# Layer norms of batches 0 to 2 placed beside the last projection of the second attention

## The chip, the cores and the metric

The kernel runs on one core of a Trainium2 chip. A core has five engines with a queue of their own each: TensorE (PE in the rows; its weight loads PEld), VectorE (DVE), ScalarE (ACT), GpSimd (POOL), and SyncE (SP), which starts transfers. They wait for each other by semaphores only. The metric is the time of one execution on the device in microseconds (us), the median of several runs.

## What is computed

A small language-model tower over 4 batches of 512 tokens with 128 features: token embedding, first attention, a layer of product-key memory, second attention, and a layer of experts, each added to the running sum `h`. The change lies between the last two:

```python
h = h + _L1_attn_ref(_layernorm(h, axis=-1), ...)   # 8 heads of 64; out @ w_out + b_out
h = h + _L1_ffn_ref(_layernorm(h, axis=-1), ...)
# in _L1_ffn_ref, x is the layer norm of h, 16 experts, k = 64
logits = jnp.einsum('bsd,de->bse', x, gate_weight)
affinity = jax.nn.softmax(logits, axis=-1).transpose(0, 2, 1)
gating, index = jax.lax.top_k(affinity, k)
x_in = jnp.take_along_axis(x[:, None, :, :], index[..., None], axis=2)
h = jax.nn.gelu(jnp.einsum('bekd,edh->bekh', x_in, w1) + b1[None, :, None, :])
x_e = jnp.einsum('bekh,ehd->bekd', h, w2) + b2[None, :, None, :]
# gating * x_e is added at the chosen tokens
```

## The kernel before

All is written by hand, one block of code per engine; the order in the code is the order in each engine's queue. `h` stays in SBUF, 16 tiles of 128 tokens; a batch (`B` = 4, `S` = 512) is four of them (`TPB`). PSUM has eight banks: 0 and 1, `quad` (2 to 5), 6 and 7.

The second attention (`attention(a1, b, ...)`) runs over 32 units of a batch, one head and 128 rows each. For a unit, TensorE makes logits (L1295), VectorE their maximum (L717), ScalarE the exponentials (L463), GpSimd the normalising product (L364); TensorE transposes (L1097), ScalarE and VectorE take the result apart into two parts (L472, and the subtraction L730), and TensorE multiplies with the values (L1109). ScalarE copies each finished head to `oT` (L477). The three first batches are in a loop. At its tail each of them contains the layer norm of the next batch: statistics on VectorE (`ln_stats`, L689 to L694) after unit 28's subtraction, the power -0.5 on GpSimd (L356, `rstd_step`), the scaling on VectorE (`ln_scale`, L701) after unit 30's, and four transposes on TensorE (`transpose_xn`, L1084, into bank 7), which ScalarE copies (L451). Then come the head projections of the next batch, and among them the output projection of the one that is done. The fourth batch is outside the loop, without a next layer norm, and its output projection (`project1(B - 1)`, L1132 and the bias L1133, into bank 6) stands alone at the end. VectorE adds it to `h` (`residual`, L747).

The expert stage begins behind that. For each batch in turn: layer norm (`lnE`), transposes into bank 7, two copies on ScalarE, into `xnT` (L651) and `xnT_all` (L652), and gate products on TensorE (L1337), which read `xnT` and write columns of bank 6. `stats`, `mv`, `rstd`, `xn` and bank 7 are there once, so a batch's scaling waits for the transposes of the one before (`ln.ps`), and transposes wait for the copies of the one before (`lnE.sb`). Behind the four batches VectorE reads the logits (L1016) and makes their softmax with an exponential on ScalarE (L654); TensorE transposes it (L1365), and VectorE finds the top 64 in eight rounds (L1032, L1034) while TensorE goes through the 16 experts of batch 0: `up` (L1344), GELU on ScalarE (L661), `down` (L1349), the result kept in `y0`. After expert `GATED` = 9 TensorE waits for the gates, transposes them (L1376), and adds one bias product (L1357) after each of the next four experts. A loop over batches 1 to 3 follows, whose results VectorE weighs and adds to `h`.

Of the kernel before, what the change touches and what calls it, by code (L numbers as in the profile page):

```python
# [13 lines left out]
def tower(nc, x_idx, val_idx, num_rows, mask_idx, event_table, value_table, tok_w1, tok_b1, tok_w2b2,  # L14
# [7 lines left out]
    P = 128  # L22
# [26 lines left out]
    GATED = 9  # L49

    with ExitStack() as ctx:
# [396 lines left out]
        def _(act):  # L448
# [5 lines left out]
            def attention(a, b, next_ln=None):  # L454
# [24 lines left out]
                for s in range(UNITS + 9):  # L479
# [7 lines left out]
                    if s == UNITS + 4 and next_ln is not None:  # L487
                        copy_xnT(next_ln, b + 1)
# [157 lines left out]
            attention(a1, B - 1)  # L646


            for b in range(B):
                act.wait_ge(lnE.ps, b + 1)  # L650
                nc.scalar.copy(xnT[:], bank[7][:, :])  # L651
                nc.scalar.copy(xnT_all[:, b * S:(b + 1) * S], bank[7][:, :]).then_inc(lnE.sb, 1)  # L652
# [31 lines left out]
        def _(dve):  # L684
# [25 lines left out]
            def attention(a, b, next_ln=None):  # L710


                m = a.mem

# [18 lines left out]
                for s in range(UNITS + 4):  # L733
# [6 lines left out]
                    if s == UNITS and next_ln is not None:  # L740
                        ln_stats(next_ln, (b + 1) * TPB, TPB)
                    if s == UNITS + 2 and next_ln is not None:
                        ln_scale(next_ln, b + 1, (b + 1) * TPB, TPB)
# [262 lines left out]
            attention(a1, B - 1)  # L1006
# [4 lines left out]
            for b in range(B):  # L1011
                layer_norm(lnE, b, b * TPB, TPB)
# [65 lines left out]
        def _(pe):  # L1078
# [8 lines left out]
            def attention(a, b, logits, next_ln=None):  # L1087
# [26 lines left out]
                for s in range(UNITS + 8):  # L1114
# [8 lines left out]
                    if s == UNITS + 3 and next_ln is not None:  # L1123
                        transpose_xn(next_ln, b + 1)

            def project(a, b, wo, bo):
# [7 lines left out]
                last.then_inc(a.proj, 1)  # L1134
# [164 lines left out]
            def project1(b):  # L1299
                pe.wait_ge(ld_wo1, 16)  # L1300
                project(a1, b, lambda g: wo1[:, g, :], bo1[:])
# [23 lines left out]
            attention(a1, B - 1, logits1)  # L1325
            project1(B - 1)


            pe.wait_ge(ld_moe, 80)
            for b in range(B):  # L1330
                if b:
                    pe.wait_ge(lnE.sb, b)
                transpose_xn(lnE, b)
                pe.wait_ge(lnE.sb, b + 1)
                for j in range(TPB):

                    last = mm(bank[6][:, (j * B + b) * NE:(j * B + b + 1) * NE], xnT[:, j * P:(j + 1) * P], gate_w[:],  # L1337
                              start=True, stop=True)
                last.then_inc(lg_ps, 1)

# [109 lines left out]
```

## Time and profile before

| | us |
|---|---|
| median of three runs | 1363.96 |
| lowest and highest | 1362.43, 1366.89 |
| the profiled execution | 1364.92 |
| its span, first to last instruction | 1363.1 |
| TensorE busy in the span | 1091.6 |
| VectorE busy in the span | 1032.9 |
| mean granted TensorE clock (1 is full) | 0.919 |

The span is what the trace covers; times in rows are microseconds from its start. A difference of two times in the trace is a difference in the same execution.

### The profile page before, as it was taken

Reading aid. Unit: us, or ns where it says so; the run is one execution under the profiler, and the core shown is the slowest. Engines: PE = TensorE matmul, PEld = TensorE weight load, DVE = VectorE, ACT = ScalarE, POOL = GpSimd, SP = SyncE. Lnnn points to the kernel's source line nnn. Section 1 sums busy time; section 2 is a strip of 40 time slices with the busy share of each in tenths; the row PEclk is TensorE's granted clock in tenths of the full one; section 3 lists DMA queues with packets and bytes.
Section 4 is the critical chain, followed back from the end, with each engine's and each line's share of the span. In section 5 each row is a group of like instructions: output and inputs, shape, how many; then the busy total and the mean of one; then the engine's idle time right before and its main releaser. Section 6 shows DMA issues by size and latency. Waiting matters only on the chain.

```text
span 1363.1 us, 24162 instructions
## 1 busy us (share of the span) xinstructions
PE 1091.6 (80%) x7848; PEld 835.8 (61%) x7848; DVE 1032.9 (76%) x2991; ACT 689.3 (51%) x1457; POOL 643.4 (47%) x530
## 2 busy tenths in 40 slices
PE   4386785867943888888888878789999898979997
PEld 2354554545532777777777778455665655656675
DVE  4697685976828999999999997387585876844587
ACT  1484674856713344344434433277484775815433
POOL 7474361743623776876677665154260542610000
PEclk9698897998977899898899989899899899978999
DMA  3300000000000000000000001100000000000000
GB/s 78 142 1 1 0 0 0 0 0 0 1 31 1 1 2 2 2 2 2 1 2 2 1 2 40 77 1 1 0 0 0 0 0 1 1 1 1 1 8 23
DMA packets 6425, 14.63 MB, mean 11 GB/s; under 512 B 1855, under 2 KB 4482, under 8 KB 5762
## 3 DMA queue, kind: packets, MB, share of 16 engines
q1 hardware_dynamic: 5314, 11.42, 2.4%
q0 software_dynamic: 1024, 2.10, 0.6%
q8 instruction: 49, 0.80, 0.3%
q14 instruction: 38, 0.31, 0.1%
HBM read 12.47 MB, written 1.05 MB: 10 GB/s over the span
## 4 chain that ended last, share of the span: by engine, by line
issue 32%; DVE 31%; PE 25%; POOL 6%; DVEq 3%; ACT 2%; POOLq 1%; DMA 0%; ACTq 0%; SPq 0%
DVE one_u L927 6%; DVE w_v L921 5%; PE quad L1349 4%; PE quad L1097 4%; PE bank L1344 4%; DVE a_eT L730 4%; DVE i L865 3%; PE quad L1109 3%; POOL wu L346 2%; DVE vals L936 2%; DVE m L858 2%; DVE bi L883 2%; POOL a_en L364 1%; DVEq L920 1%; DVE a_negmax L717 1%
## 5 line engine op out<-in xcount | busy, mean ns | idle before, releaser
L364 POOL TENSOR_TENSOR a_en<-a_e,a_rrec 128x512 f32<-128x512 f32 x256 | 265.1, 1040 | 300.7 <-DVE a_rrec L724 282.9
L717 DVE TENSOR_REDUCE a_negmax<-bank 128x1 f32<-128x512 f32 x256 | 176.1, 691 | 44.7 <-PE bank L1295 28.3
L463 ACT ACTIVATE a_e<-bank,a_negmax 128x512 f32<-128x512 f32 x256 | 176.3, 689 | 64.2 <-DVE a_negmax L717 53.6
L1097 PE MATMUL quad<-ident,a_en 128*128 128x128 f32 x1024 | 166.4, 287 | 42.1 <-DVE a_eT L730 35.2
L1097 PEld LDWEIGHTS quad<-ident,a_en 128*128 128x128 f32 x1024 | 112.4, 145 | 135.4 <-issue 121.7
L730 DVE TENSOR_TENSOR a_eT<-quad,a_eT 128x512 fp32r<-128x512 f32 x256 | 172.6, 676 | 4.5 <-ACT a_eT L472 4.3
L1109 PE MATMUL quad<-a_eT,a_v 128*128 128x512 f32 x512 | 174.1, 431 | 1.0 <-DVE a_eT L730 0.9
L396 POOL TENSOR_TENSOR vals<-relu_in,g_sb 128x512 f32<-128x512 f32 x80 | 141.3, 1792 | 40.4 <-ACT g_sb L590 21.3
L472 ACT CAST a_eT<-quad 128x512 fp32r<-128x512 f32 x256 | 148.0, 578 | 15.2 <-PE quad L1097 15.2
L1237 PE MATMUL bank<-xnT,wd 128*128 128x128 f32 x1024 | 129.0, 283 | 3.1 <-ACT relu_in L557 1.3
L1237 PEld LDWEIGHTS bank<-xnT,wd 128*128 128x128 f32 x1024 | 121.5, 195 | 8.8 <-ACT relu_in L557 8.4
L1268 PE MATMUL bank<-wu,vals 128*128 128x128 f32 x1024 | 119.3, 278 | 4.8 <-issue 4.8
L1268 PEld LDWEIGHTS bank<-wu,vals 128*128 128x128 f32 x1024 | 117.9, 195 | 4.9 <-issue 4.9
L1257 PE MATMUL quad<-w_v,one_u 128*128 128x64 f16 x2048 | 77.6, 199 | 46.5 <-DVE one_u L927 25.4
L1257 PEld LDWEIGHTS quad<-w_v,one_u 128*128 128x128 f16 x2048 | 71.0, 101 | 59.9 <-DVE one_u L927 35.0
L927 DVE TENSOR_TENSOR one_u<-iota_u,uv 128x2048 f16<-128x2048 f16 x64 | 97.4, 1580 | 0.0
L1295 PE MATMUL bank<-a_kT,a_qT 128*128 128x512 f32 x256 | 84.8, 419 | 9.3 <-DVE a_v L998 6.9
L557 ACT ACTIVATE relu_in<-bank 128x512 f32<-128x512 f32 x128 | 75.2, 596 | 24.1 <-PE bank L1237 22.4
L1349 PEld LDWEIGHTS quad<-wu,hidT 128*128 128x128 f32 x512 | 67.6, 194 | 31.4 <-issue 27.4
L1109 PEld LDWEIGHTS quad<-a_eT,a_v 128*128 128x128 f32 x512 | 79.6, 190 | 5.9 <-DVE a_eT L730 2.4
L590 ACT COPY g_sb<-quad 128x512 f32<-128x512 f32 x16 | 9.4, 587 | 138.9 <-PE quad L1257 138.9
L661 ACT ACTIVATE hidT<-bank,b1e 128x512 f32<-128x512 f32 x64 | 44.0, 687 | 62.7 <-PE bank L1344 62.4
(210 smaller groups left out, 2023.2 us busy)
## 6 DMA issues: line engine op xcount, KB each, us to landing
wd<-in_pk_down SPq DMA_DIRECT2D x1, 2048.0 KB, 8.3
wu<-in_pk_up SPq DMA_DIRECT2D x1, 2048.0 KB, 12.8
wu<-in_moe_w SPq DMA_DIRECT2D x2, 1024.0 KB
out<-h SPq DMA_DIRECT2D x4, 256.0 KB, 2.3
wd<-in_num_rows SPq DMA_DIRECT2D x1, 512.0 KB
vals<-in_pk_wqT SPq DMA_DIRECT2D x1, 512.0 KB, 3.7
vals<-in_pk_keys SPq DMA_DIRECT2D x1, 512.0 KB, 4.6
wd<-in_a_wq SPq DMA_DIRECT2D x1, 512.0 KB
```

What stands on the lines that cost most here:

```text
L364: nc.gpsimd.tensor_tensor(m.en[:, s % 3, :], m.e[:, s % 3, :], m.rrec[:, s % 4:s % 4 + 1].to_broadcast([P, S]), ALU.mult).then_inc(a.nr, 1)
L396: nc.gpsimd.tensor_tensor(*weigh_args(t, c, k, g_sb[:, slot, :])).then_inc(vals_pool, 1)
L463: nc.scalar.activation(m.e[:, s % 3, :], bank[LOGITS[s % 3]][:, :], ACT.Exp, bias=m.negmax[:, s % 4:s % 4 + 1], accum_out=m.rowsum[:, s % ...
L472: nc.scalar.copy(m.eT[:, hd % 2, 0, :, j * P:(j + 1) * P], bank[2 + s % 2].rearrange("p (c n) -> p c n", c=TPB)).then_inc(a.hi, 1)
L717: V.tensor_reduce(m.negmax[:, s % 4:s % 4 + 1], bank[LOGITS[s % 3]][:, :], AX.X, ALU.max, negate=True).then_inc(a.mx, 1)
L730: V.tensor_tensor(part[:, 1], bank[2 + s % 2].rearrange("p (c n) -> p c n", c=TPB), part[:, 0].bitcast(F32), ALU.subtract).then_inc(a.lo, 1)
L927: V.tensor_tensor(one_u[:, c * n:(c + 1) * n], iota_u[:].unsqueeze(1).to_broadcast([P, n, NU, 2]), token_pairs(uv[:, t % 2, 0, c * GT:(c + ...
L1097: last = tp(bank[2 + s % 2][:, c * P:(c + 1) * P], m.en[:, s % 3, c * P:(c + 1) * P], ident[:])
L1109: last = mm(bank[4 + g % 2], m.v[:, c, hd, :], m.eT[:, hd % 2, part, c, :], start=(hd % a.group == 0 and c == 0 and part == 0), stop=(hd % ...
L1237: last = mm(bank[g % 2][:, q * P:(q + 1) * P], wd[:, IG * g + q, :], xnT_tile(t), start=True, stop=True)
L1257: made = mm(quad[:, 2 * (c % 2) + i // half_pair, cols], one_u[:, pair // 2, :, pair % 2], w_v[:, pair // 2, k, :, :, pair % 2].rearrange( ...
L1268: last = mm(bank[6][:, 0:D], vals[:, v, :], wu[:, v, :], start=(v == 0), stop=(v == NV - 1))
```

## The change

The last attention gets a next layer norm as well, that of batch 0 for the experts. The layer norms of batches 1 and 2 follow on VectorE's queue directly behind the attention, ahead of the residual of the last batch. On TensorE their transposes stand inside the last output projection, after its first and its third block. The layer norm of batch 3 stays behind the residual. ScalarE makes one copy per batch, straight into `xnT_all`, and the gate products read that. Those of batches 0 and 1 stand behind a wait for the residual, which still reads bank 6; then come the transposes of batch 3, and the products of batches 2 and 3. `GATED` becomes 10. GpSimd's and SyncE's queues are the same.

```diff
     LOGITS = (0, 1, 6)
-    GATED = 9
+    GATED = 10
...
-            def attention(a, b, next_ln=None):
+            def attention(a, b, next_ln=None, n=None, dst=None):
...
                     if s == UNITS + 4 and next_ln is not None:
-                        copy_xnT(next_ln, b + 1)
+                        copy_xnT(next_ln, b + 1 if n is None else n, dst=dst)
...
                 heads1(b + 1)
-            attention(a1, B - 1)
-
-
-            for b in range(B):
-                act.wait_ge(lnE.ps, b + 1)
-                nc.scalar.copy(xnT[:], bank[7][:, :])
-                nc.scalar.copy(xnT_all[:, b * S:(b + 1) * S], bank[7][:, :]).then_inc(lnE.sb, 1)
+            attention(a1, B - 1, lnE, 0, xnT_all[:, 0:S])
+
+
+            for b in range(1, B):
+                copy_xnT(lnE, b, dst=xnT_all[:, b * S:(b + 1) * S])
             act.wait_ge(lg_exp_in, 1)
...
-            def attention(a, b, next_ln=None):
+            def attention(a, b, next_ln=None, n=None):
                 m = a.mem
+                n = b + 1 if n is None else n
...
                     if s == UNITS and next_ln is not None:
-                        ln_stats(next_ln, (b + 1) * TPB, TPB)
+                        ln_stats(next_ln, n * TPB, TPB)
                     if s == UNITS + 2 and next_ln is not None:
-                        ln_scale(next_ln, b + 1, (b + 1) * TPB, TPB)
+                        ln_scale(next_ln, n, n * TPB, TPB)
...
                 heads1(b + 1, b)
-            attention(a1, B - 1)
+            attention(a1, B - 1, lnE, 0)
+            layer_norm(lnE, 1, TPB, TPB)
+            layer_norm(lnE, 2, 2 * TPB, TPB)
             residual(a1, B - 1)
...
-            for b in range(B):
-                layer_norm(lnE, b, b * TPB, TPB)
+            layer_norm(lnE, B - 1, (B - 1) * TPB, TPB)
             V.memset(aff, 0.0)
...
-            def attention(a, b, logits, next_ln=None):
+            def attention(a, b, logits, next_ln=None, n=None):
...
                     if s == UNITS + 3 and next_ln is not None:
-                        transpose_xn(next_ln, b + 1)
-
-            def project(a, b, wo, bo):
+                        transpose_xn(next_ln, b + 1 if n is None else n)
+
+            def project(a, b, wo, bo, beside=None):
...
                     last = mm(dst, ones[0:1, :], bo, start=False, stop=True)
-                last.then_inc(a.proj, 1)
+                    if j == TPB - 1:
+                        last.then_inc(a.proj, 1)
+                    elif beside is not None:
+                        beside(j)
...
-            def project1(b):
+            def project1(b, beside=None):
                 pe.wait_ge(ld_wo1, 16)
-                project(a1, b, lambda g: wo1[:, g, :], bo1[:])
+                project(a1, b, lambda g: wo1[:, g, :], bo1[:], beside)
...
                 heads1(b + 1, b)
-            attention(a1, B - 1, logits1)
-            project1(B - 1)
-
-
-            pe.wait_ge(ld_moe, 80)
-            for b in range(B):
-                if b:
+            def transpose_early(j):
+                if j in (0, 2):
+                    b = 1 + j // 2
                     pe.wait_ge(lnE.sb, b)
-                transpose_xn(lnE, b)
+                    transpose_xn(lnE, b)
+
+            attention(a1, B - 1, logits1, lnE, 0)
+            project1(B - 1, transpose_early)
+
+
+            def gate(b):
                 pe.wait_ge(lnE.sb, b + 1)
...
-                    last = mm(bank[6][:, (j * B + b) * NE:(j * B + b + 1) * NE], xnT[:, j * P:(j + 1) * P], gate_w[:],
-                              start=True, stop=True)
+                    last = mm(bank[6][:, (j * B + b) * NE:(j * B + b + 1) * NE],
+                              xnT_all[:, b * S + j * P:b * S + (j + 1) * P], gate_w[:], start=True, stop=True)
                 last.then_inc(lg_ps, 1)
+
+            pe.wait_ge(ld_moe, 80)
+            pe.wait_ge(a1.add, B)
+            gate(0)
+            gate(1)
+            pe.wait_ge(lnE.sb, B - 1)
+            transpose_xn(lnE, B - 1)
+            gate(2)
+            gate(3)
```

The order of the queues, built from both programs (`[waits ...]` names the semaphores that an instruction waits for, and line numbers are each program's own).

VectorE at the end of batch 3's attention, before: the last subtractions of the exponentials, then the residual and the layer norms.

```order
L730 TENSOR_TENSOR a_eT<-quad,a_eT 128x4x128 [waits a1_expT_hi] x4
L747 TENSOR_TENSOR h<-h,bank 128x512 [waits a1_projected]
L689 BN_STATS stats<-h 128x6 x4
L692 BN_AGGR mv<-stats 128x2 x4
L694 TENSOR_SCALAR veps<-mv 128x4
L701 TENSOR_SCALAR xn<-h,mv,rstd 128x128 [waits lnE_rstd_ready]
L701 TENSOR_SCALAR xn<-h,mv,rstd 128x128 x3
```

The same place after:

```order
L729 TENSOR_TENSOR a_eT<-quad,a_eT 128x4x128 [waits a1_expT_hi]
L687 BN_STATS stats<-h 128x6 x4
L690 BN_AGGR mv<-stats 128x2 x4
L692 TENSOR_SCALAR veps<-mv 128x4
L729 TENSOR_TENSOR a_eT<-quad,a_eT 128x4x128 [waits a1_expT_hi] x2
L699 TENSOR_SCALAR xn<-h,mv,rstd 128x128 [waits lnE_rstd_ready]
L699 TENSOR_SCALAR xn<-h,mv,rstd 128x128 x3
L729 TENSOR_TENSOR a_eT<-quad,a_eT 128x4x128 [waits a1_expT_hi]
L687 BN_STATS stats<-h 128x6 x4
L690 BN_AGGR mv<-stats 128x2 x4
L692 TENSOR_SCALAR veps<-mv 128x4
L699 TENSOR_SCALAR xn<-h,mv,rstd 128x128 [waits lnE_rstd_ready,lnE_xnT_in_psum]
```

Statistics and scaling of batch 0 now stand among the last subtractions, and batch 1 directly behind them. Batch 2 follows in the same five rows, and then:

```order
L746 TENSOR_TENSOR h<-h,bank 128x512 [waits a1_projected]
L687 BN_STATS stats<-h 128x6 x4
L690 BN_AGGR mv<-stats 128x2 x4
L692 TENSOR_SCALAR veps<-mv 128x4
L699 TENSOR_SCALAR xn<-h,mv,rstd 128x128 [waits lnE_rstd_ready,lnE_xnT_in_psum]
```

So the residual stands behind three layer norms, and one layer norm behind it.

TensorE, the second half of the last projection and what comes behind it, before (`wo`, `bo`: weights and bias of the projection):

```order
L1132 MATMUL bank<-wo,oT 128x128 x8
L1133 MATMUL bank<-bo,ones 128x128
L1132 MATMUL bank<-wo,oT 128x128 x8
L1133 MATMUL bank<-bo,ones 128x128
L1084 MATMUL bank<-ident,xn 128x128 [waits lnE_xn_ready,ld_moe]
L1084 MATMUL bank<-ident,xn 128x128 x3
L1337 MATMUL bank<-gate_w,xnT 128x16 [waits lnE_xnT_in_sbuf]
L1337 MATMUL bank<-gate_w,xnT 128x16 x3
L1084 MATMUL bank<-ident,xn 128x128 [waits lnE_xn_ready,lnE_xnT_in_sbuf]
L1084 MATMUL bank<-ident,xn 128x128 x3
```

The projection from its first block on, after:

```order
L1132 MATMUL bank<-wo,oT 128x128 [waits a1_outT_in_sbuf,ld_wo1]
L1132 MATMUL bank<-wo,oT 128x128 x7
L1133 MATMUL bank<-bo,ones 128x128
L1084 MATMUL bank<-ident,xn 128x128 [waits lnE_xn_ready,lnE_xnT_in_sbuf]
L1084 MATMUL bank<-ident,xn 128x128 x3
L1132 MATMUL bank<-wo,oT 128x128 x8
L1133 MATMUL bank<-bo,ones 128x128
L1132 MATMUL bank<-wo,oT 128x128 x8
L1133 MATMUL bank<-bo,ones 128x128
L1084 MATMUL bank<-ident,xn 128x128 [waits lnE_xn_ready,lnE_xnT_in_sbuf]
L1084 MATMUL bank<-ident,xn 128x128 x3
L1132 MATMUL bank<-wo,oT 128x128 x8
```

and directly behind it:

```order
L1133 MATMUL bank<-bo,ones 128x128
L1342 MATMUL bank<-gate_w,xnT_all 128x16 [waits lnE_xnT_in_sbuf,a1_h_added,ld_moe]
L1342 MATMUL bank<-gate_w,xnT_all 128x16 x3
L1342 MATMUL bank<-gate_w,xnT_all 128x16 [waits lnE_xnT_in_sbuf]
L1342 MATMUL bank<-gate_w,xnT_all 128x16 x3
L1084 MATMUL bank<-ident,xn 128x128 [waits lnE_xn_ready,lnE_xnT_in_sbuf]
L1084 MATMUL bank<-ident,xn 128x128 x3
L1342 MATMUL bank<-gate_w,xnT_all 128x16 [waits lnE_xnT_in_sbuf]
L1342 MATMUL bank<-gate_w,xnT_all 128x16 x3
L1342 MATMUL bank<-gate_w,xnT_all 128x16 [waits lnE_xnT_in_sbuf]
L1342 MATMUL bank<-gate_w,xnT_all 128x16 x3
L1358 MATMUL bank<-xnT_all,wu 128x512
```

Two groups of transposes moved in between the blocks of the projection (that of batch 0 stands further up, in the attention), and all gate products stand behind it, on both sides of the one group of transposes that is left there.

## Rows read from the trace of the kernel before

**Rows 1.** The page: busy us (share of the span) xinstructions.

```profile
PE 1091.6 (80%) x7848; PEld 835.8 (61%) x7848; DVE 1032.9 (76%) x2991; ACT 689.3 (51%) x1457; POOL 643.4 (47%) x530
```

**Rows 2.** Instructions in time: start, us, engine line op, operands [idle before <-releaser].

```profile
1199.25 2.02 PE L1132 MATMUL bank<-wo,oT 128*128 128x128 f32 x16 [0.77 <-ACT oT L477]
...
1208.38 0.48 PE L1133 MATMUL bank<-bo,ones 1*128 1x128 f32 x2
1208.91 0.69 DVE L747 TENSOR_TENSOR h<-h,bank 128x512 f32<-128x512 f32 x1 [12.59 <-PE bank L1133]
1209.69 0.87 DVE L689 BATCH_NORM_STATS2 stats<-h 128x6 f32<-128x128 f32 x4
...
1212.38 1.12 DVE L701 TENSOR_SCALAR xn<-h,mv,rstd 128x128 f32<-128x128 f32 x4 [1.12 <-POOL rstd L356]
...
1213.64 1.09 PE L1084 MATMUL bank<-ident,xn 128*128 128x128 f32 x4 [4.78 <-DVE xn L701]
```

**Rows 3.** Chain of waits, 1214 to 1242 us: start, us, what.

```profile
1214.77 0.59 ACT xnT L651
1215.36 0.50 ACT xnT_all L652
...
1215.89 1.89 PE bank L1337 x8
...
1227.86 1.91 PE bank L1337 x8
...
1229.78 0.43 DVE logit L1016
...
1232.99 1.12 PE bank L1365 x4
...
1239.93 0.86 PE bank L1344 x2
1240.79 0.89 PE quad L1349 x8
```

**Rows 4.** Stretches: A:B us; busy (x) PE, PEld, DVE, ACT, POOL; granted clock; DMA.

```profile
1208.90:1211.40 2.50, 0.00 (x0) 0.00 (x0) 2.11 (x10) 0.00 (x0) 0.06 (x1) 1.00 0.00 0
1211.50:1229.70 18.20, 11.41 (x49) 9.83 (x49) 8.94 (x44) 4.29 (x8) 3.87 (x4) 0.50 0.00 0
...
1233.00:1238.70 5.70, 5.70 (x16) 3.96 (x17) 3.59 (x7) 2.52 (x4) 0.00 (x0) 0.50 0.01 3
1238.80:1256.00 17.20, 17.20 (x103) 12.76 (x101) 9.31 (x19) 12.64 (x20) 0.00 (x0) 1.00 0.00 0
```

**Rows 5.** Instructions in time, tail of batch 2's attention.

```profile
1107.89 2.04 POOL L364 TENSOR_TENSOR a_en<-a_e,a_rrec 128x512 f32<-128x512 f32 x2 [0.68 <-DVE a_rrec L724]
...
1109.67 0.86 DVE L689 BATCH_NORM_STATS2 stats<-h 128x6 f32 x4
...
1113.38 0.69 DVE L730 TENSOR_TENSOR a_eT<-quad,a_eT 128x512 fp32r<-128x512 f32 x1
...
1113.53 0.66 PE L1084 MATMUL bank<-ident,xn 128*128 128x128 f32 x4
...
1114.20 2.13 PE L1109 MATMUL quad<-a_eT,a_v 128*128 128x512 f32 x8
```

**Rows 6.** Instructions in time, tail of batch 3's attention.

```profile
1191.42 2.04 POOL L364 TENSOR_TENSOR a_en<-a_e,a_rrec 128x512 f32<-128x512 f32 x2 [0.68 <-DVE a_rrec L724]
...
1196.37 2.11 PE L1109 MATMUL quad<-a_eT,a_v 128*128 128x512 f32 x8 [0.47 <-DVE a_eT L730]
```

**Rows 7.** Instructions in time: the gates, and the transposes that wait for them.

```profile
1248.30 0.69 DVE L1038 TENSOR_TENSOR gT<-gT,affT 128x512 f32<-128x512 f32 x1
...
1253.78 0.60 PE L1376 MATMUL bank<-ident,gT 128*128 128x128 f32 x4
```

**Rows 8.** TensorE behind three idle pieces, and the clock of stretches after them.

```profile
974.68 1.87 PE L1295 MATMUL bank<-a_kT,a_qT 128*128 128x512 f32 x6 [1.86 <-DVE a_v L998]
...
976.00:982.50 6.50, 5.99 (x20) 3.90 (x19) 4.17 (x11) 4.74 (x12) 4.07 (x4) 0.50 0.00 0
...
1059.73 1.60 PE L1295 MATMUL bank<-a_kT,a_qT 128*128 128x512 f32 x6 [1.84 <-DVE a_v L998]
...
1061.30:1068.00 6.70, 5.91 (x20) 4.35 (x20) 4.37 (x12) 4.85 (x13) 4.18 (x5) 0.50 0.00 0
...
1144.70 1.65 PE L1295 MATMUL bank<-a_kT,a_qT 128*128 128x512 f32 x6 [1.62 <-DVE a_v L998]
...
1144.80:1150.00 5.20, 3.95 (x19) 2.60 (x20) 3.44 (x8) 3.43 (x9) 2.77 (x3) 1.00 0.00 0
```

## The prediction, made before the changed kernel ran

> **What bounds the kernel now.** I began with the page: TensorE is busy for 80% of a span of 1363.1 us, so no engine is full everywhere, and a change of this size has to be read in its own stretch [rows 1]. The views of 1190 to 1240 us come next, where the second attention ends and the expert stage begins. The last projection runs from 1199.25 to 1208.86 us, in four blocks of 16 matmul records and two bias records, 9.61 us in all, so 2.40 us a block [rows 2]. Behind it nothing overlaps. VectorE adds the residual at 1208.91, then computes the statistics of batch 0, GpSimd raises them to the power (VectorE waits 1.12 us for it), VectorE scales, and TensorE gets its first transpose at 1213.64, after 4.78 us without work [rows 2]. The chain of waits then repeats one pattern four times, once a batch, of which the first and the last are shown: transposes, two copies on ScalarE, gate products (1.89 us for four, x8 in the records) [rows 3]. Batches 1 to 3 follow in 3.99 us each (1227.86 - 1215.89, over three), and the layer norms of these batches lie beside that pattern; it is transposes, copies and gate products that end last. The logits are read at 1229.78, and their softmax ends when TensorE transposes it at 1232.99 [rows 3]. From there on the stage is one unbroken TensorE sequence of 1.75 us per expert (0.86 up, 0.89 down) [rows 3], so what is won before it moves the end of the kernel with it.
>
> The table of stretches adds the clock [rows 4]. The granted clock is 1.00 until 2.5 us behind the projection, 0.50 (the 1.2 GHz level instead of 2.4 GHz) all through transposes and gate products, and 1.00 again only 5.7 us after the softmax. So the stretch between projection and experts runs at the low level, and it stands between two long waits.
>
> **Removed.** From the end of the projection to the end of the last gate product: 1229.77 - 1208.86 = 20.91 us [rows 2, 3]. Of this all goes that belongs to batches 0 to 2, as far as something else covers it.
>
> **What stays behind the projection.** The residual, the layer norm of batch 3 and its transposes still hang on it, as batch 0's did: 4.78 us of wait, then 1.10 us for four transposes at the low clock. Products of batches 0 and 1 now stand in front of those transposes. They wait for the residual, because they write the bank that it reads: about 0.8 us behind the projection, then 2 x 0.99 us at full clock (a block's 16 matmul records take 2.02 us, 8 gate records half of that, less a little [rows 2]), or 2 x 1.89 at the low one. Both fit into the 4.78 us (0.8 + 3.8 = 4.6), so they cost nothing; without that cover they would cost 2.0 to 3.8 us. Products of batch 2 follow at once and hide the one copy that ScalarE still has to make for batch 3 (0.59 us). Products of batch 3 end the stretch. Sum at the low clock: 4.78 + 1.10 + 0.05 + 1.89 + 1.89 = 9.71 us instead of 20.91, so **-11.2 us**. The second copy and the extra reader of `xnT` that go are inside this sum; on their own they would have been worth 0.50 us in each batch [rows 3], but for batch 3 the products of batch 2 lie over them.
>
> **What the moved work costs in front.** Batch 0's layer norm now sits in the tail of the last attention, just as the layer norm for the heads of batch 3 sits in the tail of batch 2's attention. That tail is in the trace, and so is the last one, which has no layer norm [rows 5, 6]. I lay both on the last pair of GpSimd products (1107.89 and 1191.42, 83.53 us apart). With the layer norm the last eight attention records end at 1114.20 + 2.13 = 1116.33, which is 1199.86 in the later frame; without it they ended at 1196.37 + 2.11 = 1198.48. The reason is the row of VectorE: statistics at 1109.67 stand in front of two subtractions of the exponentials, and the scaling in front of the last one (1113.38), for which TensorE waits. The four transposes (0.66 us at 1113.53) fall into that wait. So the projection starts **+1.38 us** later.
>
> Inside the projection TensorE now does two groups of four transposes, after blocks 0 and 2: 2 x 0.65 = **+1.30 us**, at full clock [rows 5]. They have to be ready: VectorE is free at 1113.38 + 0.69 + 83.53 = 1197.6, statistics and power of batch 1 take 2.69 us (1209.69 to 1212.38 in rows 2), scaling 1.12, so batch 1 is ready at 1201.5, while TensorE comes to it at 1200.63 + 2.40 = 1203.0. Slack 1.5 us. Batch 2 needs `xn` free, so it waits for these transposes (1203.7), and is ready at 1205.3; TensorE comes to it at 1208.5. Slack 3.2 us. ScalarE copies between them and has nothing else to do. The residual stands behind both layer norms on VectorE, and those are over 6 us before the projection ends, so nobody waits for that. GpSimd is through with its products at 1191.42 + 2.04 = 1193.46, over 1 us before the statistics of batch 0 are there; no product or DMA stands behind its loop of four.
>
> **No cost.** The gate products read the same numbers from another tile, with equal shapes. `GATED` 10 moves the transposes of the gates one expert back: the gates are ready at 1248.30 + 0.69 = 1248.99, and TensorE came for them at 1253.78, so the wait was empty by 4.8 us, and with 10 by 6.5 [rows 7]. Their rows stay as many, and the four bias terms end one expert before the last. Were the clock to return at once after the softmax, TensorE would be there 2.8 us earlier and still find them.
>
> **Sum.** -11.2 + 1.38 + 1.30 = **-8.5 us**. The profiled execution took 1364.92 us (span 1363.1), the median of the three runs is 1363.96, so 1.0 us lower; a difference carries over, and the forecast is 1363.96 - 8.5 = 1355.5 us.
>
> **The clock, weighed.** The sum has the low level in it, and the new program shortens the wait that brought it: behind the projection TensorE now idles 0.8 us, works, idles 4.78 - 0.8 - 2.0 = 2.0 us in front of the transposes, and later some 2.3 us during the softmax (3.21 us from 1229.78 to 1232.99, less 0.86 for the first expert product at full clock). In the trace idle pieces of 1.86 and 1.84 us were followed by a fall: after 974.68 and 1059.73 the clock is 1.00 and then 0.50 for 6.5 us; one of 1.62 us, before 1144.70, was not [rows 8]. So 2.0 and 2.3 us, close together, should bring it down once at least, and I take the low level from in front of batch 3's transposes. The Trainium skill, TensorE: Matmul & The Clock Gate, section "Why this matters for your kernels", asks only that TensorE not stand still between bursts for longer than a length which neither of these pieces reaches; by that rule the clock stays at its full level, and the time is that of the first rival. Rows 8 speak against the page here.
> How long the low level lasts past the softmax is open from both sides. Before it was 5.7 us, all of it TensorE work that took twice its time, worth 2.8 us. A return at once gives -2.8; the longest stretch that rows 8 show, 6.7 us, gives +0.5. The position of a fall or a rise is not something that this change sets, so I take 5.7 again, as the nearest row of the same work.
>
> **Rivals.**
> 1. *The clock never falls.* Transposes 0.66 instead of 1.10, gate products 0.99 twice instead of 1.89, so 2.2 us, and 2.8 us behind the softmax: -8.5 - 2.2 - 2.8 = -13.5, 1350.5 us. If it falls only in the softmax, -10.7, 1353.3 us. For: both idle pieces are far shorter than 4.78. Against: rows 8.
> 2. *The tail of the attention pays more.* VectorE's queue holds statistics, a wait for GpSimd and the scaling in front of subtractions, and in the last batch there is no following projection of heads to take up slack. If a whole layer norm shows (3.8 us from 1209.69 to the end of the scaling, [rows 2]) and not 1.38, then -8.5 + 2.4 = -6.1, 1357.9 us. For: each subtraction is waited for. Against: the tail in rows 5 has the same queue, and pays 1.38.
> 3. *Slower: the projection stalls and loses the clock.* TensorE takes its queue in order, so blocks 1 to 3 stand behind batch 1's transposes. If batch 1 is not ready 1.5 us after my time, TensorE idles; if it idles by some 1.85 us more, the clock falls as in rows 8, and the remaining 7.2 us of projection take 14.4. Cost 1.85 + 7.2 + 0.4 for the second transposes = 9.5, so +1.0 net, 1365.0 us, and over that for each us of lateness. It decides from 3.4 us of lateness in all. Nothing in the trace makes the same chain of 3.8 us take 7.2, so this is remote.
> 4. *It does not do what it says.* The end of the logits might hang on something else than the four batches. The chain has no other link there [rows 3], so no change, 1364 us, is left a small chance.
>
> **How the numbers follow.** Forecast 0.70 (1355.5, its own range 1353.5 to 1357 by the bounds of the clock); rival 1 at full 0.07 and with a late fall 0.08; rival 2 0.10; rival 3 0.02; rival 4 0.03. The three runs of before spread by 4.5 us, and a median by perhaps 1, so I widen a little: 1351.5 to 1358.2 leaves out the full-clock case, rivals 3 and 4, and some spread of the rest. A difference of 0.3%, 4.1 us, is about what a measurement of this kernel can tell from none. Faster than 1359.9: forecast and rivals 1 and 2, 0.94 (with 0.01 off for spread). Same: 0.04. Slower: 0.02.
>
> **What would show it.** In the changed profile: the last projection starts about 1.4 us later and lasts 10.9 instead of 9.6 us, with no idle piece inside it; from its end to the last gate product 9.7 us, with 4.8 us from its end to batch 3's transposes; the granted clock 0.50 before these transposes and until some 5.7 us after the softmax; the wait for the gates still empty; 1.75 us for each expert as before. A stretch of 7.5 us instead of 9.7 says that the clock held. A projection that starts over 2 us later says rival 2, an idle piece inside it rival 3. I am wrong altogether if the softmax does not come about 8.5 us earlier, or if the time from there to the end grows.

## The result and the profile after

The changed kernel took 1354.97 us (median of five runs, 1353.12 to 1356.15) against 1363.96 us: 0.9928 of before, with a 95% interval of 0.991 to 0.9947. The same two kernels on another occasion gave 1355.27 against 1364.23 us, 0.9931 (0.9915 to 0.9946). So it is faster by 0.7%, 9.0 us by the medians on both occasions, where 8.5 were forecast.

The timeline of the changed kernel from the last attention to the experts (columns as in [rows 2]):

```profile
1189.52 2.04 POOL L364 TENSOR_TENSOR a_en<-a_e,a_rrec 128x512 f32<-128x512 f32 x2 [0.67 <-DVE a_rrec L723]
...
1195.16 0.66 PE L1084 MATMUL bank<-ident,xn 128*128 128x128 f32 x4
...
1195.76 2.09 PE L1109 MATMUL quad<-a_eT,a_v 128*128 128x512 f32 x8
...
1198.62 2.02 PE L1132 MATMUL bank<-wo,oT 128*128 128x128 f32 x16 [0.77 <-ACT oT L477]
...
1200.99 0.66 PE L1084 MATMUL bank<-ident,xn 128*128 128x128 f32 x4
...
1201.48 1.95 PE L1132 MATMUL bank<-wo,oT 128*128 128x128 f32 x16
...
1206.17 0.66 PE L1084 MATMUL bank<-ident,xn 128*128 128x128 f32 x4
...
1206.66 1.95 PE L1132 MATMUL bank<-wo,oT 128*128 128x128 f32 x16
...
1208.54 0.48 PE L1133 MATMUL bank<-bo,ones 1*128 1x128 f32 x2
1209.07 0.69 DVE L746 TENSOR_TENSOR h<-h,bank 128x512 f32<-128x512 f32 x1 [5.78 <-PE bank L1133]
...
1209.86 1.93 PE L1342 MATMUL bank<-gate_w,xnT_all 128*128 128x16 f32 x16 [0.83 <-issue]
...
1213.87 1.09 PE L1084 MATMUL bank<-ident,xn 128*128 128x128 f32 x4 [2.08 <-DVE xn L699]
```

The groups of transposes (L1084) now stand in the attention's tail and between the blocks of the projection, and no row of the projection has an idle piece in front but its first. The row at 1213.87 shows where the rest of the time is: TensorE idle for 2.08 us, waiting for batch 3's layer norm.

The chain of waits behind it, for [rows 3]:

```profile
1213.87 1.09 PE bank L1084 x4
1214.96 3.24 PE bank L1342 x16
...
1218.22 0.42 DVE logit L1016
...
1221.42 1.12 PE bank L1379 x4
...
1228.39 0.86 PE bank L1358 x2
1229.25 0.89 PE quad L1363 x8
```

One group of transposes and two sets of gate products, where there were four of each, and the same 3.20 us of softmax. An expert takes 0.86 + 0.89 us as before. And the clock, for [rows 4]:

```profile
1209.10:1213.50 4.40, 1.93 (x16) 1.86 (x16) 2.97 (x14) 0.00 (x0) 1.01 (x1) 1.00 0.00 0
1213.60:1221.40 7.80, 6.21 (x22) 4.66 (x22) 2.97 (x8) 2.29 (x3) 0.00 (x0) 0.50 0.00 1
1221.50:1227.10 5.60, 5.60 (x16) 3.89 (x17) 3.59 (x7) 2.45 (x4) 0.00 (x0) 0.50 0.01 3
1227.30:1244.00 16.70, 16.70 (x100) 12.36 (x99) 9.23 (x18) 12.14 (x19) 0.00 (x0) 1.00 0.00 0
```

It fell at about 1213.5, just ahead of the last transposes, and came back 5.8 us behind the start of the softmax's transposes (1221.42).

The two executions had drifted apart by 1.9 us when they reached this place, for reasons that lie before it, where the programs are the same. The differences are therefore counted from a mark that both have, the start of the last pair of GpSimd products (1191.42 and 1189.52). Times are in us:

| stretch | before | after | difference | forecast |
|---|---|---|---|---|
| mark to first projection product | 7.83 | 9.10 | +1.27 | +1.38 |
| projection | 9.61 | 10.40 | +0.79 | +1.30 |
| its end to the reading of the logits | 20.92 | 9.20 | -11.72 | -11.2 |
| logits to the softmax's transposes | 3.21 | 3.20 | 0.0 | 0 |
| from there to the end | 130.11 | 129.88 | -0.2 | 0 |
| sum | | | -9.9 | -8.5 |

### The profile page after: what moved, and what is told of

Same layout as the page of the kernel before. It is cut to its first block, busy times and chain, and to the rows that moved or that the text cites. A ratio compares the mean times of both kernels' runs of the same rounds, so it can differ in the third digit from the quotient of the medians.

```text
span 1351.3 us, 24158 instructions
## 1 busy us (share of the span) xinstructions
PE 1084.5 (80%) x7848; PEld 830.7 (61%) x7848; DVE 1033.9 (77%) x2991; ACT 686.1 (51%) x1453; POOL 643.4 (48%) x530
## 4 chain that ended last, share of the span: by engine, by line
issue 32%; DVE 32%; PE 24%; POOL 6%; DVEq 3%; ACT 2%; POOLq 1%; DMA 0%; ACTq 0%; SPq 0%
DVE one_u L926 6%; DVE w_v L920 5%; PE quad L1363 4%; PE quad L1097 4%; PE bank L1358 4%; DVE a_eT L729 4%; DVE i L864 3%; PE quad L1109 3%; POOL wu L346 2%; DVE vals L935 2%; DVE m L857 2%; DVE bi L882 2%; POOL a_en L364 1%; DVEq L919 1%; DVE a_negmax L716 1%
## 5 line engine op out<-in xcount | busy, mean ns | idle before, releaser
L1298 PE MATMUL bank<-a_kT,a_qT 128*128 128x512 f32 x256 | 81.4, 404 | 9.6 <-DVE a_v L997 6.9
```

## Experiments

All are read by the same stretches, in one profiled execution each. Two times are given: from the mark (the last pair of GpSimd products) to the softmax's transposes, 31.90 us in the changed kernel, and from there to the end, 129.88 us. In a second trace of the changed kernel they were 31.93 and 129.83 us. That is much closer than whole times, which spread by 3 to 5 us and more, and on some occasions lay 8 to 12 us higher for all kernels. The second time moves with the clock, though: it depends on how long the low level lasts behind the softmax.

### GATED back to 9

```diff
-    GATED = 10
+    GATED = 9
```

> The changed kernel with GATED back at 9; nothing else differs. My theory: the gates are ready before TensorE asks for them at 9 as at 10, so the time from the softmax's transposes to the end stays at 129.9 us (within 0.5), and the transposes of the gates start 20.8 us behind the softmax's transposes with no wait of over 0.3 us in front, instead of 22.5. Rival: the top-64 search is late for expert 9 now, TensorE waits there, and the stretch to the end grows by that wait, 1 us or more.

To the softmax's transposes 31.93 us, from there to the end 128.89, so 1.0 us less than with 10. The gates and the transposes that wait for them:

```profile
1248.72 0.69 DVE L1038 TENSOR_TENSOR gT<-gT,affT 128x512 f32<-128x512 f32 x1
...
1252.99 0.60 PE L1390 MATMUL bank<-ident,gT 128*128 128x128 f32 x4
```

Ready 3.6 us early, and no idle piece, so 9 would have done as well. My 0.5 us was missed by the clock, not by `GATED`:

```profile
1233.50:1236.60 3.10, 3.10 (x9) 2.06 (x10) 1.34 (x3) 1.49 (x3) 0.00 (x0) 0.50 0.02 5
1236.70:1254.00 17.30, 17.30 (x102) 12.76 (x102) 11.53 (x24) 12.54 (x21) 0.00 (x0) 1.00 0.00 0
```

It came back 3.3 us behind the softmax's transposes here (1233.41) and not 5.8. Expert products take twice their time at the low level (1.71 us for 0.86 in the chain of the changed kernel), so half of the difference is gained, 1.3 us, which is more than the whole 1.0 us.

The low stretch is as long as in the changed kernel, 13.7 us in both; it lies 2.5 us earlier. It begins at about 1223.0, while TensorE is in the gate products of batches 0 and 1, whose row is 2.50 us long for 1.93 in the changed kernel:

```profile
1221.83 2.50 PE L1342 MATMUL bank<-gate_w,xnT_all 128*128 128x16 f32 x16 [0.83 <-issue]
1225.85 1.09 PE L1084 MATMUL bank<-ident,xn 128*128 128x128 f32 x4 [1.51 <-DVE xn L699]
```

```profile
1220.90:1222.90 2.00, 1.17 (x11) 1.10 (x10) 1.69 (x7) 0.00 (x0) 0.00 (x0) 1.00 0.00 0
1223.10:1225.80 2.70, 1.24 (x6) 1.13 (x6) 1.37 (x7) 0.00 (x0) 1.01 (x1) 0.50 0.01 3
```

So in this trace the clock fell before the idle piece in front of batch 3's transposes, and nothing was late by it: the transposes started 4.85 us behind the projection, as with 10.

### Two copies again

```diff
                 act.wait_ge(ln.ps, i + 1)
+                if ln is lnE:
+                    nc.scalar.copy(xnT[:], bank[7][:, :])
                 nc.scalar.copy(xnT[:, 0:n] if dst is None else dst,
```

> The changed kernel with the second copy on ScalarE put back: for each batch bank 7 is copied into xnT and then into xnT_all; gate products still read xnT_all. My theory: both copies lie beside projection blocks or the gate products of batch 2, so from the last pair of GpSimd products to the softmax's transposes it stays at 31.9 us within 0.2. Rival: the copies are on the path behind the last transposes, and the stretch grows by 0.5 us (by 2.0 us if each batch pays).

31.93 us to the softmax's transposes. The copies lie beside other work in every batch, as forecast. From there to the end it was 129.52 us, with the clock back after 5.0 us instead of 5.8; half of that is the 0.4 us that it is less than in the changed kernel.

### One copy, in the order of before

```diff
             for b in range(B):
                 act.wait_ge(lnE.ps, b + 1)
-                nc.scalar.copy(xnT[:], bank[7][:, :])
                 nc.scalar.copy(xnT_all[:, b * S:(b + 1) * S], bank[7][:, :]).then_inc(lnE.sb, 1)
...
-                    last = mm(bank[6][:, (j * B + b) * NE:(j * B + b + 1) * NE], xnT[:, j * P:(j + 1) * P], gate_w[:],
+                    last = mm(bank[6][:, (j * B + b) * NE:(j * B + b + 1) * NE], xnT_all[:, b * S + j * P:b * S + (j + 1) * P], gate_w[:],
```

> The kernel before with that part of the change alone: one copy per batch straight into xnT_all, gate products read it, all four layer norms still behind the residual. My theory: each of the four rounds of transposes, copy and gate products loses the 0.50 us of the second copy, so from the last pair of GpSimd products to the softmax's transposes 41.6 - 4 x 0.50 = 39.6 us, or somewhat more if the layer norm chain of 3.7 us per batch becomes what ends last: the period goes from 3.99 towards 3.5, so the chain of 3.72 to 3.79 stops it, and three periods give 3 x 0.22 and the last 0.50, 40.4 us. Time within 0.3% of before. Rival: the copy is not on the path at all, 41.6 us.

40.49 us, 1.08 less than the 41.57 of before, where the closer of the two forecasts said 40.4. Whole time 0.9986 of before (0.9964 to 1.0007). Two rounds of its timeline:

```profile
1227.54 1.09 PE L1083 MATMUL bank<-ident,xn 128*128 128x128 f32 x4
...
1229.31 1.89 PE L1336 MATMUL bank<-gate_w,xnT_all 128*128 128x16 f32 x8 [0.68 <-ACT xnT_all L651]
1230.08 1.11 DVE L700 TENSOR_SCALAR xn<-h,mv,rstd 128x128 f32<-128x128 f32 x4 [1.20 <-POOL rstd L356]
...
1231.34 1.09 PE L1083 MATMUL bank<-ident,xn 128*128 128x128 f32 x4
```

The period is 3.79 us instead of 3.99, and the scalings on VectorE, which wait for GpSimd's `rstd`, follow each other at 3.79 us: with one copy the layer norms end last. This part of the change is worth 1.1 us alone and nothing within the rest. The reordering is what brings the time.

### All three early layer norms beside the projection

```diff
-            attention(a1, B - 1, lnE, 0)
+            attention(a1, B - 1)
+            layer_norm(lnE, 0, 0, TPB)
             layer_norm(lnE, 1, TPB, TPB)
...
-                if j in (0, 2):
-                    b = 1 + j // 2
-                    pe.wait_ge(lnE.sb, b)
-                    transpose_xn(lnE, b)
+                if j:
+                    pe.wait_ge(lnE.sb, j)
+                transpose_xn(lnE, j)
```

> The changed kernel with batch 0's layer norm taken out of the tail of the attention: all three layer norms follow the last subtraction on VectorE, and their transposes stand behind blocks 0, 1 and 2 of the last projection. My theory: the tail is 1.27 us shorter (last pair of GpSimd products to the first projection product 7.83 us as before the change, not 9.10), the projection holds three groups of transposes at 0.49 us, some 0.4 us more than now, and does not stall, so from that pair to the softmax's transposes 31.9 - 1.27 + 0.4 = 31.0 us. Rival: the layer norms are late now, TensorE stands still inside the projection, and the stretch is longer than 31.9 us.

31.56 us: 0.34 less than the changed kernel, not the 0.9 forecast. The tail is 7.83 us again, so the layer norm there costs what the comparison of two tails had said. The projection grew to 11.33 us, for two reasons, of which one is the rival's:

```profile
1220.48 1.11 DVE L699 TENSOR_SCALAR xn<-h,mv,rstd 128x128 f32<-128x128 f32 x4 [1.19 <-POOL rstd L356]
1220.77 0.48 PE L1134 MATMUL bank<-bo,ones 1*128 1x128 f32 x2
1221.74 0.63 PE L1085 MATMUL bank<-ident,xn 128*128 128x128 f32 x4 [0.49 <-DVE xn L699]
```

The third layer norm is 0.49 us late for its place behind block 2; the rest is one more group of transposes. The clock stayed up through the projection.

### Idle time filled with useless products

```diff
+            def fill(n):
+                for _ in range(n):
+                    mm(bank[1][:, :], w1e[:, 0, :], xnT_all[:, 0:S], start=True, stop=True)
...
             gate(1)
+            fill(2)
             pe.wait_ge(lnE.sb, B - 1)
...
             up(0, 0)
+            fill(2)
             pe.wait_ge(aff_rdy, 1)
```

> The changed kernel with idle TensorE given useless work of the real kind (the first expert product again, into bank 1 which nobody reads yet): two products behind the gate products of batches 0 and 1, two behind the first expert product. They measure what the low clock costs. My theory: the clock stays at 1.00 across both waits. From the last transposes to the logits 2.6 us instead of 4.35, from the last pair of GpSimd products to the softmax's transposes 30.2 instead of 31.9 us, from there to the end 127.1 instead of 129.9; 4.5 us in all. Rival: the fall does not come from idle time here, the clock falls all the same, the fillers run at half speed, and the stretch gets longer, 32 us or more.

The second run has the first `fill` only.

> The changed kernel with the filler products behind the gate products of batches 0 and 1 only. My theory: the last transposes and gate products run at full clock, 30.2 us to the softmax's transposes; in the wait of the softmax, about 2.3 us idle, the clock falls, and the time from there to the end is 129 to 130.5 us as before. Rival: the wait of the softmax is too short to bring the clock down, and the end comes after 127.1 us.

With both, 29.96 us to the softmax's transposes and 127.06 behind: 4.76 us less than the changed kernel's 31.90 and 129.88, with more work on TensorE. Whole time 0.9922 of before (0.9901 to 0.9943), on an occasion on which the changed kernel was not run, so its gain over that one is read from the trace. The whole times do not confirm all of it: 9.0 us and 4.8 together would be 0.990 of before, just outside the interval, and the profiled execution was the fastest of four (1359.05 us; the slowest took 1363.58). The medians leave some 2 us. The rows of the fillers, and the table of stretches, in which the clock did not fall:

```profile
1222.29 1.96 PE L1340 MATMUL bank<-xnT_all,wu 128*128 128x512 f32 x4
...
1227.68 1.88 PE L1340 MATMUL bank<-xnT_all,wu 128*128 128x512 f32 x4
```

```profile
1219.70:1224.50 4.80, 3.74 (x20) 2.47 (x21) 3.29 (x15) 0.00 (x0) 1.01 (x1) 1.00 0.00 2
1224.60:1230.10 5.50, 4.96 (x26) 3.18 (x26) 2.69 (x7) 2.28 (x3) 0.00 (x0) 1.00 0.00 0
```

With the first alone, 29.95 us to the softmax's transposes (1226.60); then it fell after all:

```profile
1223.00:1226.60 3.60, 1.31 (x6) 0.49 (x5) 2.37 (x6) 1.72 (x3) 0.00 (x0) 1.00 0.00 0
1227.80:1231.00 3.20, 3.20 (x11) 2.33 (x10) 2.87 (x6) 1.35 (x3) 0.00 (x0) 0.50 0.00 0
1231.30:1240.00 8.70, 8.70 (x51) 6.37 (x50) 7.90 (x18) 6.31 (x10) 0.00 (x0) 1.00 0.00 0
```

That cost 1.64 us, 128.70 instead of 127.06, for 3.4 us at 0.50. So the fall does not need both waits: with the first filled it came behind the softmax's, which left TensorE idle for 2.29 us. By the difference of the traces, the low clock costs 1.9 us in the changed kernel up to the softmax's transposes and 2.8 behind them.

### Gate products of batch 2 ahead of batch 3's transposes

```diff
             gate(1)
-            pe.wait_ge(lnE.sb, B - 1)
+            gate(2)
             transpose_xn(lnE, B - 1)
-            gate(2)
             gate(3)
```

> The changed kernel with the gate products of batch 2 ahead of batch 3's transposes too, where TensorE idles 2.08 us. My theory: behind the last transposes only the copy and one set of gate products are left, so with the low clock 3.7 us from the last transposes to the logits, as in the kernel with one copy and the old order, instead of 4.35, and 31.25 us to the softmax's transposes; if the shorter idle piece, 1.1 us, does not bring the clock down, 2.6 us, and 30.1. Rival: nothing gained, since the copy stands open now (0.65 us) where the products hid it, 31.9 us.

31.20 us, and 3.72 from the last transposes to the logits: the first forecast, at the low clock. The copy stands open and costs 0.67 us, but the products of batch 2, which stand elsewhere now, took 1.3 us in its place. The clock fell at about 1224.4, where the gate products ended and the idle piece of 1.10 us began.

```profile
1225.53 1.11 PE L1084 MATMUL bank<-ident,xn 128*128 128x128 f32 x4 [1.10 <-DVE xn L699]
1226.68 0.59 ACT L451 COPY xnT_all<-bank 128x512 f32<-128x512 f32 x1 [7.47 <-PE bank L1084]
1227.32 1.89 PE L1342 MATMUL bank<-gate_w,xnT_all 128*128 128x16 f32 x8 [0.67 <-ACT xnT_all L451]
```

### The second expert product ahead of the softmax's transposes

```diff
             up(0, 0)
+            up(0, 1)
             pe.wait_ge(aff_rdy, 1)
...
-                if e + 1 < NE:
+                if 1 < e + 1 < NE:
                     up(0, e + 1)
```

> The changed kernel with the second expert product ahead of the softmax's transposes instead of behind them. My theory: TensorE idles 1.35 us there; the product takes 1.71 us at the low clock, so the transposes come 0.36 us later (32.3 us) and the end 1.71 us earlier after them (128.2 us), 1.35 us in all. Rival: what follows waits for ScalarE (table load, GELU, copy of the transposed softmax) and not for TensorE, and nothing is gained in all.

32.06 us and 127.19 us, together 2.5 us less than the changed kernel. Not all of this is the edit: the clock came back 2.1 us behind the softmax's transposes, 3.7 us earlier than in the changed kernel, which is worth 1.85 by half. What is left, 0.7 us, is about half of the 1.35 us forecast and near the 0.86 us of one expert product at full clock. It speaks against the rival, which had nothing, but it is a remainder in one trace. The softmax's transposes came 0.16 us later than in the changed kernel, not 0.36.

### All of it together

The changed kernel once more, for comparison in the same rounds:

> The changed kernel unchanged, for its ratio to the kernel before on this chip. My theory: the stretches of its trace read -9.7 us up to the softmax and -0.2 behind it, so 0.993 of before. Rival: the 9 us of the first comparison were partly the spread of both kernels, and the ratio is nearer 0.996.

And the reorderings that had helped, in one kernel. VectorE's layer norm of batch 0 moves behind the attention as well; on TensorE:

```diff
             def transpose_early(j):
-                if j in (0, 2):
-                    b = 1 + j // 2
-                    pe.wait_ge(lnE.sb, b)
-                    transpose_xn(lnE, b)
+                if j == 2:
+                    return
+                if j:
+                    pe.wait_ge(lnE.sb, j)
+                transpose_xn(lnE, j)
...
             pe.wait_ge(ld_moe, 80)
+            pe.wait_ge(lnE.sb, B - 2)
+            transpose_xn(lnE, B - 2)
             pe.wait_ge(a1.add, B)
             gate(0)
             gate(1)
-            pe.wait_ge(lnE.sb, B - 1)
-            transpose_xn(lnE, B - 1)
             gate(2)
+            transpose_xn(lnE, B - 1)
             gate(3)
...
             up(0, 0)
+            up(0, 1)
             pe.wait_ge(aff_rdy, 1)
...
-                if e + 1 < NE:
+                if 1 < e + 1 < NE:
                     up(0, e + 1)
```

> The changed kernel with what the runs so far point to: batch 0's layer norm behind the attention, transposes of batches 0 and 1 behind the first two blocks of the projection and those of batch 2 behind its last block (beside the residual), gate products of batches 0 to 2 ahead of batch 3's transposes, and the second expert product ahead of the softmax's transposes. My theory: 7.83 us to the projection, 10.4 in it, 4.85 from its end to the last transposes; then 3.7 us to the logits at the low clock and 2.4 at the full one, 3.2 more to the softmax's transposes, so 30.0 or 28.7 us instead of 31.9. Behind that 126.2 us at full clock, up to 128.2 at the low one, instead of 129.9. In all 3.5 to 7 us less than the changed kernel. Rival: with less TensorE work left behind the projection, the softmax and layer norm chains on VectorE bound it, and nothing over 2 us is gained.

The combined kernel took 1348.74 us (1348.16 to 1349.53), 0.9885 of before (0.9869 to 0.9901), where the changed kernel in the same rounds took 1355.27, 0.9931. The intervals are apart: the combined one is 6.5 us faster by the medians. By the trace it took 29.65 us to the softmax's transposes and 126.51 behind, 5.6 us less.

```profile
1210.04 2.85 PE L1344 MATMUL bank<-gate_w,xnT_all 128*128 128x16 f32 x24 [0.19 <-DVE h L746]
1214.01 0.73 PE L1085 MATMUL bank<-ident,xn 128*128 128x128 f32 x4 [1.12 <-DVE xn L699]
1215.42 1.89 PE L1344 MATMUL bank<-gate_w,xnT_all 128*128 128x16 f32 x8 [0.68 <-ACT xnT_all L451]
1217.14 3.76 PE L1361 MATMUL bank<-xnT_all,wu 128*128 128x512 f32 x4
1220.69 0.90 PE L1383 MATMUL bank<-ident,aff 128*128 128x128 f32 x4
```

Transposes at 1214.01 still began at full clock (0.73 us), the gate products behind them ran at the low one. That lasted until 0.6 us behind the start of the softmax's transposes:

```profile
1214.50:1221.20 6.70, 6.03 (x17) 3.53 (x16) 2.37 (x6) 2.95 (x4) 0.00 (x0) 0.50 0.00 0
1221.40:1230.00 8.60, 8.60 (x52) 6.40 (x51) 7.09 (x15) 6.63 (x11) 0.00 (x0) 1.00 0.01 2
```

Of the 5.6 us, 2.3 lie in front of the softmax's transposes and 3.4 behind; of these 3.4, the earlier return of the clock (0.6 us for 5.8) is 2.6 us by half, and the rest is about one expert product (0.86). Whether the reordering or chance placed the return there is not shown: one execution of this kernel was traced. The four whole times lie within 1.4 us.

With one useless product in the wait that is left:

```diff
             gate(2)
+            mm(bank[1][:, :], w1e[:, 0, :], xnT_all[:, 0:S], start=True, stop=True)
             transpose_xn(lnE, B - 1)
```

> The combined kernel with one useless product (the first expert product, into bank 1) in front of batch 3's transposes. My theory: it only matters if the clock falls in the combined kernel; it stays at 1.00 here to the end of the stage, 28.7 us to the softmax's transposes and 126.2 behind it. Rival: the product delays the transposes, and the stretch grows by up to 0.9 us.

31.77 and 127.30 us: worse by 2.9 us than the combined kernel, and the rival was right in kind and too small. Not all of this is the product's doing, for the clock fell 3.0 us sooner than in the combined kernel, before the useless product was reached, so that it ran at half speed and delayed the transposes, which started 6.51 us behind the projection instead of 4.75:

```profile
1207.00:1209.90 2.90, 2.90 (x22) 2.44 (x20) 0.93 (x4) 0.00 (x0) 0.00 (x0) 1.00 0.00 0
1210.00:1212.10 2.10, 1.91 (x16) 1.67 (x17) 1.92 (x9) 0.59 (x1) 0.00 (x0) 1.00 0.00 0
1212.30:1225.70 13.40, 12.73 (x41) 8.93 (x42) 4.53 (x13) 4.07 (x6) 1.01 (x1) 0.50 0.01 2
```

## Why the prediction was right, point by point

The mechanism held. That 9.0 us by the medians lie so near to the 8.5 is in part luck: by the stretches 9.9 us were won, and 1.1 us of the difference are terms that the sum had too large.

**What bounds, and what was removed.** Right. Behind the projection only batch 3's layer norm, one group of transposes and two sets of gate products were left, and the stretch fell from 20.92 to 9.20 us. The wait for the residual and the products of batches 0 and 1 cost nothing: 4.85 us from the projection's end to the last transposes, for the 4.78 of before. The products took 1.93 us from 0.84 us behind the projection, as the sum had them.

**Terms of the sum that were mis-sized.** Two, both the same way. The two groups of transposes inside the projection were put at 2 x 0.65 us and cost 0.79 in all. A group's row is 0.66 us long, but the block behind it starts 0.49 us after the group's start (1200.99 and 1201.48, 1206.17 and 1206.66), and the 16 records of that block take 1.95 us for 2.05. And from the last transposes to the logits the sum had 1.10 + 0.05 + 1.89 + 1.89 = 4.93 us, where the trace has 4.35 (1213.87 to 1218.22): here too rows overlap that the sum had end to end, so that two sets of gate products in a row took 3.24 us in the chain. Together this is 1.1 us of the 1.2 by which the sum up to the softmax's transposes was short (-9.67 for -8.5).

**The tail of the attention.** +1.27 for +1.38. The comparison of two tails was good to 0.1 us, and the kernel without this layer norm in the tail got exactly this back. Rival 2 is out.

**The clock.** The level was right: 0.50 from in front of batch 3's transposes to 5.8 us behind the start of the softmax's. The reason given for it, the idle piece of 2.0 us (2.08 in the trace), is not shown. This is where the clock fell and came back in all traces of this order, fall in us behind the projection's end, return and rest in us behind the start of the softmax's transposes:

| kernel | fall | TensorE then | return | rest |
|---|---|---|---|---|
| changed | 4.5 | idle since 2.8 | 5.8 | 129.88 |
| changed, second trace | 4.4 | idle since 2.8 | 5.7 | 129.83 |
| three layer norms beside the projection | 4.7 | idle since 2.8 | 6.0 | 130.03 |
| two copies | 3.8 | idle since 2.8 | 5.0 | 129.52 |
| `GATED` 9 | 2.0 | in gate products | 3.3 | 128.89 |
| batch 2's gate products ahead | 3.6 | at their end | 5.6 | 129.84 |
| second expert product ahead | 4.4 | idle since 2.8 | 2.1 | 127.19 |
| combined | 5.2 | in transposes | 0.6 | 126.51 |
| combined with a useless product | 2.2 | in gate products | 2.3 | 127.30 |

In three of the nine traces the clock fell before the idle piece in front of the last transposes, or just as it began. So it fell in every kernel that had no filler, and rival 1 is out, but not by that idle piece alone; what does it stays open. The rule of the Trainium skill (TensorE: Matmul & The Clock Gate, "Why this matters for your kernels") that the prediction weighed, which would have kept the clock at its full level, did not hold here: the longest idle piece between the end of the projection and the last transposes was 2.08 us, and the clock fell in it.

That the return came 5.8 us behind, where 5.7 was taken, is luck. The first five rows of the table have the same instructions from the projection's end up to the softmax (two copies apart, for which nobody waits), and returns from 3.3 to 6.0 us, worth over 1 us of the time. I had called the position of the return something that the change does not set, and that is as much as I can say of it.

**GATED 10.** No cost, and no use either: at 9 there are 3.6 us to spare.

**Rival 3 and rival 4.** No row of the projection shows an idle piece in the changed kernel. One of 0.49 us appeared only where all three layer norms were put beside it, and the clock did not fall in the projection. Rival 4 is out with the softmax's transposes 9.7 us earlier.

**What remains open.** The two medians differ by 9.0 us and the stretches by 9.9; the ratios allow 7 to 12, so nothing has to be explained there. What brings the clock down is open, above all in `GATED` 9 and in the combined kernel with the useless product, where TensorE had idled for 0.83 and 0.19 us only since the projection.

## What to carry over

Where one engine waits for a chain that each batch goes through, look for batches whose inputs are ready long before, and give their steps the cover of a stretch in which other engines idle; what must stay behind (here one batch of four) sets the new time. Cost a group of short products that is put between others by the distance from its start to the next one's start (0.49 us here), not by its row's duration (0.66). Order what is left by what can fill a wait: the edits of the combined kernel changed only the place of work that was there already, and brought 6.5 us on top of the first 9, of which some 2.6 us came with an earlier return of the clock. A stretch of a few us whose clock can change has to be compared with the clock beside it: `GATED` 9 looked 1.0 us better and was not.

## What the hardware showed that I had not expected

TensorE need not idle for long for its clock to fall. In the combined kernel with the filler it fell at about 1212.2 us; since the projection's end at 1209.98 TensorE had stood still for 0.19 us only, had done a group of transposes, and was in gate products (128x16, from 1210.76) when it fell. In `GATED` 9 it fell in such products too, after 0.83 us of idle time. With fillers behind two sets of those products instead of three, it stayed up through the same wait, in two traces. The fillers stand 2.6 us behind the projection's end, and the fall of `GATED` 9 came at 2.0, so it is not shown that they hold the clock up in every execution.

A fall can cost more than the idle time that it is seen beside: in the trace with filler products in both waits, 4.76 us less were spent, although the fillers had added rows of 1.96 and 1.88 us.
